# A four-layer graph network on one core: the first layer written out tile by tile, with the adjacency work begun behind the load of x

## The reference

```python
node_att = softmax(x @ node_w, axis=0)
h = x @ edge_w
e = where(adj > 0, h @ h.T, -9e15)
output = adj * (node_att * softmax(e, axis=1)) @ (x @ weight) + bias
```

## Time and profile before

| | us |
|---|---|
| median of 3 runs | 870.79 (870.46 to 871.27) |
| the profiled execution, its own time | 870.08 |
| its span in the trace | 868.3 |
| PE busy | 792.3 (91%) |
| DVE busy | 460.1 (53%) |
| ACT busy | 334.0 (38%) |
| POOL busy | 113.0 (13%) |
| mean granted TensorE clock | 0.977 |

### The profile page before, as it was taken

The page is one execution under the profiler, slowest core; times in us unless marked ns, Lnnn a source line. Parts: engine busy times, 40 slices in busy tenths (PEclk is TensorE's granted clock), DMA queues, the critical chain, the costliest instruction groups (busy, mean ns, idle before and its releaser), DMA issues.

```text
span 868.3 us, 12739 instructions
## 1 busy us (share of the span) xinstructions
PE 792.3 (91%) x4264; PEld 521.0 (60%) x4264; DVE 460.1 (53%) x956; ACT 334.0 (38%) x531; POOL 113.0 (13%) x232
## 2 busy tenths in 40 slices
PE   5948899999969999999997999999998999998997
PEld 5936566666548687768683564556654455465343
DVE  4663667667757768787876347312226021111655
ACT  3455555555425445454554124313335131222200
POOL 1010111111254001010101112000000100000343
PEclk9979999999978999999999999999999999999999
DMA  4149999999920000000002000000000000000011
GB/s 127 35 105 231 215 231 227 231 232 235 190 49 1 13 1 2 1 0 0 0 0 73 7 0 1 1 0 0 0 0 25 1 1 0 0 0 1 18 36 43
DMA packets 114863, 50.61 MB, mean 58 GB/s; under 512 B 103568, under 2 KB 109840, under 8 KB 114832
## 3 DMA queue, kind: packets, MB, share of 16 engines
q1 hardware_dynamic: 114832, 50.22, 25.3%
HBM read 22.95 MB, written 2.10 MB: 29 GB/s over the span
## 4 chain that ended last, share of the span: by engine, by line
PE 45%; issue 24%; SPq 8%; DMA 6%; ACT 6%; DVE 6%; POOL 4%; ACTq 0%; POOLq 0%; DVEq 0%
PE ps L633 10%; PE ps L753 10%; PE ps L731 8%; PE ps L781 7%; DMA adjf<-in_adj 5%; SPq L337 5%; PE ps L762 3%; PE ps L718 3%; SPq L327 2%; PE ps L522 2%; ACT em L819 2%; POOL x L464 2%; DVE em L1076 1%; ACT adjb L814 1%; PE ps L546 1%
## 5 line engine op out<-in xcount | busy, mean ns | idle before, releaser
L633 PE MATMUL ps<-adjT,x 128*128 (+1 forms) x768 | 173.5, 380 | 7.4 <-DVE x L1285 3.8
L633 PEld LDWEIGHTS ps<-adjT,x 128*128 128x128 f16 x768 | 71.6, 98 | 92.9 <-issue 5.6
L573 PE MATMUL ps<-sup,supf 128*128 128x512 f16 x256 | 85.8, 385 | 2.8 <-DMA supf<-pl 2.8
L658 PE MATMUL ps<-H_hi,es_hi 128*128 128x258 f32 x256 | 76.4, 298 | 9.1 <-DVE es_lo L1024 6.0
L1024 DVE TENSOR_TENSOR hh_lo<-hf,hh_hi 128x512 fp32r<-128x512 f32 x32 | 22.2, 692 | 116.6 <-ACT hf L970 116.6
L753 PE MATMUL ps<-adjT,G 128*128 x384 | 83.6, 379 | 0.4 <-ACT hf L970 0.4
L562 PE MATMUL ps<-hT_hi,hst_hi 128*128 128x512 f32 x128 | 54.2, 423 | 22.6 <-DVE mx L1076 14.4
L658 PE MATMUL ps<-H_hi,es_lo 128*128 128x258 f32 x256 | 72.5, 283 | 0.0
L658 PE MATMUL ps<-H_lo,es_hi 128*128 128x258 f32 x256 | 72.3, 283 | 0.0
L575 PE MATMUL ps<-sup,supf 128*128 128x256 f16 x256 | 70.6, 276 | 0.0
L753 PEld LDWEIGHTS ps<-adjT,G 128*128 128x128 f16 x384 | 37.2, 98 | 45.4 <-issue 0.9
(11 more groups left out here) (203 smaller groups left out, 1480.6 us busy)
## 6 DMA issues: line engine op xcount, KB each, us to landing
adjf<-in_adj SPq DMA_DIRECT2D x32, 512.0 KB, 4.7
x<-in_x SPq DMA_DIRECT2D x4, 512.0 KB, 8.2
out<-adjf SPq DMA_DIRECT2D x16, 128.0 KB, 1.7
adjf<-in_L_gnn_W SPq DMA_DIRECT2D x1, 1024.0 KB, 6.2
W1f<-in_L_gnn_W SPq DMA_DIRECT2D x1, 512.0 KB, 3.6
adjf<-in_L_gnn_W SPq DMA_DIRECT2D x1, 512.0 KB, 3.7
we<-in_L_gnn_edge_w SPq DMA_DIRECT2D x1, 256.0 KB, 3.8
w0x<-in_L_gnn_weight SPq DMA_DIRECT2D x1, 256.0 KB, 4.0
```

Source lines behind the costliest of these rows:

```text
L573: ins = mm(bank(6 + u), PT(HI, u)[:, jt, :], sup[:, jt, :], start=(jt == 0), stop=False, skip_group_check=True)
L633: ins = mm(bank(4 + f), x16[:, part, jt, f * P:(f + 1) * P], adjT[:, jt, bass.ds(b * CB, CB)], start=(jt == 0 and part == HI), stop=(jt == ...
L658: ins = mm(bank(k, D + 2), es[p][:, jt % RE, k * P:(k + 1) * P], H[q][:, jt, :], start=(jt == 0 and (p, q) == (HI, HI)), stop=(jt == T - 1 ...
```

## The change

- P0 is reordered: transposes and h of a block alternate, so that a block's h follows when its x has landed; the scores of row 0 stand ahead of the 16 support groups, the scores of row 1 behind them.
- x is loaded ahead of the support weights, the node column and the bias; only `we` (for h) stands between its first and second quarter.
- The adjacency loads are issued right behind x, no longer after the 32 groups. ACT casts rows 0 and 1 behind the h groups, row 2 behind the support groups, and from then on row t+3 in row t. `adjb` has four rows (AB) instead of two, `ph` and `pl` one each instead of two.
- The staging copies of h on POOL are gone: S(t) reads its stationary side from hT itself.
- PT has room of its own. `supf` and the transposed x lie in what are the later blocks of adjT, so the adjacency turns from row 4 on wait for the scaled support.
- adjT is [128, B, T, 512], block by block, for all layers.
- The loops of layer 0 are written out on all engines; the last aggregation loops over blocks of four tiles instead of pairs.

Shapes and the list of the first groups:

```diff
+    AB = 4
...
+    P0 = [(what, b, f) for what, b in (("turn", 0), ("turn", 1), ("h", 0), ("turn", 2), ("h", 1), ("turn", 3), ("h", 2),
+                                       ("h", 3)) for f in range(KD)]
...
-        adjT = sb(ctx, "adjT", [P, T, N], BF16)
+        before = ExitStack()
+        sb(before, "first_block", [P, T, CB], BF16)
+        supf = sb(before, "supf", [P, T, D])
+        xT0 = pair(before, "xT0", [P, KD, N])
+        before.close()
+        adjT = sb(ctx, "adjT", [P, B, T, CB], BF16)
...
+        turned = sb(lay0, "turned", [P, 4, T, P], F16)
...
-        ph, pl = (sb(main0, name, [P, 2, N], F16) for name in ("ph", "pl"))
-        adjb = sb(main0, "adjb", [P, 2, N], BF16)
+        ph, pl = (sb(main0, name, [P, N], F16) for name in ("ph", "pl"))
+        adjb = sb(main0, "adjb", [P, AB, N], BF16)
```

SP:

```diff
                 if c == 0:
-                    sp.dma_start(we[:, :, :], w_tiles(edge_in)).then_inc(w0_landed, 16)
-                    sp.dma_start(w0x[:, :, 0:D], w_tiles(w0_in)).then_inc(w0_landed, 16)
-                    sp.dma_start(w0x[:, :, D:D + 1], w_tiles(node_in)).then_inc(w0_landed, 16)
-                    sp.dma_start(brow[:, :], vec_row(b0_in)).then_inc(w0_landed, 16)
+                    sp.dma_start(we[:, :, :], w_tiles(edge_in)).then_inc(we_landed, 16)
+            sp.dma_start(w0x[:, :, 0:D], w_tiles(w0_in)).then_inc(w0_landed, 16)
+            sp.dma_start(w0x[:, :, D:D + 1], w_tiles(node_in)).then_inc(w0_landed, 16)
+            sp.dma_start(brow[:, :], vec_row(b0_in)).then_inc(w0_landed, 16)
...
+            def turn_adj(t):
...
                 sp.wait_ge(adj_cast, 2 * t + 2)
+                if t >= TB:
+                    sp.wait_ge(sup_lo, TB)
+                sp.dma_start_transpose(adjT[:, t // TB, :, t % TB * P:(t % TB + 1) * P], adjb[:, t % AB, :]) \
+                    .then_inc(adjT_landed[t % AB], 16)
+
+            def turn_p(t, part):
+
+                sp.wait_ge((p_hi, p_lo)[part], 2 * t + 2)
+                wait_from(sp, pv_mm, t - 1)
+                sp.dma_start_transpose(PT(part, t % 2), (ph, pl)[part][:, :]).then_inc(PT_landed[part], 16)
...
-            sp.wait_ge(p0_lo, P0_GROUPS)
             load_adj(0)
             load_adj(1)
-            transpose_adj(0, 0)
-            sp.wait_ge(sup_lo, TB)
...
+            turn_adj(0)
+            load_adj(2)
+            turn_adj(1)
+            load_adj(3)
+            turn_adj(2)
+            turn_p(0, HI)
+            turn_p(0, LO)
+            turn_p(1, HI)
+            load_adj(4)
+            turn_adj(3)
+            load_adj(5)
+            turn_p(1, LO)
+            turn_adj(4)
+            for t in range(2, T):
+                turn_p(t, HI)
+                turn_p(t, LO)
+                if t + 4 < T:
+                    load_adj(t + 4)
+                if t + 3 < T:
+                    turn_adj(t + 3)
```

PE (`group0(n)` is group n of P0 or, from P0_SUP on, a support group):

```diff
-                            ins = mm(bank(c), hst[p][:, u, k, :], hT[q][:, k, c * CB:(c + 1) * CB],
+                            ins = mm(bank(c), hT[p][:, k, t * P:(t + 1) * P], hT[q][:, k, c * CB:(c + 1) * CB],
...
-            scores(0, 0, range(B))
-            scores(1, 1, range(B))
+            for n in range(P0_SUP):
+                group0(n)
+            scores(0)
+            for n in range(P0_SUP, P0_GROUPS):
+                group0(n)
+            scores(1)
+            pe.wait_ge(p0_lo, P0_GROUPS)
             pe.wait_ge(sup_lo, TB)
...
+            for t in range(2, T):
+                scores(t)
+                weighted(t - 2)
+            weighted(T - 2)
+            weighted(T - 1)
```

ACT:

```diff
+            def cast(t):
+
+                if t == 2:
+                    act.wait_ge(p0_lo, P0_GROUPS)
+                if t >= AB:
+                    act.wait_ge(adjT_landed[t % AB], 16 * (t // AB))
+                    act.wait_ge(fill_ready, t - AB + 1)
...
+            for n in range(P0_SUP):
+                group0(n)
+            cast(0)
+            cast(1)
+            for n in range(P0_SUP, P0_SUP + 2):
+                group0(n)
+            exp_row(0)
+            for n in range(P0_SUP + 2, P0_SUP + 6):
+                group0(n)
+            p_high(0)
+            for n in range(P0_SUP + 6, P0_GROUPS):
+                group0(n)
+            cast(2)
             act.wait_ge(node_neg, 1)
             run(nl[:, :], nl[:, :], ACT.Exp, bias=nst[:, 2:3], accum_out=nst[:, 3:4]).then_inc(node_exp, 1)
-            round0(0, 0, 0)
             act.wait_ge(scale_ready, 1)
             for c in range(TB):
...
+            exp_row(1)
+            p_high(1)
+            cast(3)
+            cast(4)
+            for t in range(2, T):
+                exp_row(t)
+                p_high(t)
+                if t + 3 < T:
+                    cast(t + 3)
```

DVE:

```diff
+            for n, (what, b, f) in enumerate(P0):
+                if n == P0_SUP - 2:
+                    dve.wait_ge(w0_landed, 48)
...
             maxima(0, 0)
+            for t in range(T):
+                n = P0_SUP + t
+                dve.wait_ge(p0_hi, n + 1)
...
+            nc.vector.reduce_max(g1[:, 0:1], smax[:, :], AX_X).then_inc(tmax_ready, 1)
+            p_low(0, 0)
+            dve.wait_ge(node_gmax, 1)
+            ts(nst[:, 2:3], nst[:, 1:2], -1.0, None, ALU.mult).then_inc(node_neg, 1)
             scale_of(1)
+            maxima(1, 1)
+            for c in range(TB):
...
+            p_low(1, 1)
...
+            for t in range(2, T):
+                round0(t)
```

Every reader of adjT, here one of them:

```diff
-                                 adjT[:, jt, bass.ds(b * CB, CB)], start=(jt == 0 and part == HI),
+                                 adj(b, jt), start=(jt == 0 and part == HI),
```

More of the change, by code:

```diff
@@ L438, in _ @@
             nc.gpsimd.partition_all_reduce(nst[:, 4:5], nst[:, 3:4], P, RADD).then_inc(node_sum, 1)
[L439 removed]
             bias_x(0, 0)
[L441 removed]
             bias_x(1, 1)
[L443 to L450 removed]
+            for t in range(T - 2):
                 norm_factor(t, t % 2)
@@ L528, in _, with group0 @@
             pe.wait_ge(const_ready, 3)
-            for n in range(P0_GROUPS):
+            def group0(n):
                 if n >= 4:
@@ L550, in _, with scores @@
                     ins = project(bank(to, D + 2), xT0, slice(t * P, (t + 1) * P), w0s, D + 2)
                 ins.then_inc(p0_mm, 1)
-            def scores(t, u, banks):
-                pe.wait_ge(h_staged, 2 * (t + 1))
-                for c in banks:
+            def scores(t):
+                if t == 0:
+                    pe.wait_ge(p0_lo, P0_SUP)
+                for c in range(B):
                     if c % 2 == 0:
@@ L683, in _ @@
             pe.wait_ge(H_ready, 2)
-            for u in range(2):
-                pe.wait_ge(adjT_landed[u], 8 * T)
+            for k in range(AB):
+                pe.wait_ge(adjT_landed[k], 16 * (T // AB))
             block1(0)
@@ L752, in hidden2 @@
                     for part in (HI, LO):
-                        ins = mm(bank(4 + o), g16(jt, part, o * P, P), adjT[:, jt, bass.ds(b * CB, CB)],
+                        ins = mm(bank(4 + o), g16(jt, part, o * P, P), adj(b, jt),
                                  start=(jt == 0 and part == HI), stop=(jt == T - 1 and part == LO))
@@ L761, in _ @@
                     for part in (HI, LO):
-                        ins = mm(bank(4 + o), g16(jt, part, o * P, P), adjT[:, jt, 0:CB],
+                        ins = mm(bank(4 + o), g16(jt, part, o * P, P), adj(0, jt),
                                  start=(jt == 0 and part == HI), stop=(jt == T - 1 and part == LO))
@@ L780, in out3 @@
                         pe.wait_ge(c3_lo, T + jt + 1)
-                    ins = mm(bank(u), adjT[:, jt, bass.ds(t * P, P)], f16[:, jt, :], start=(jt == 0),
+                    ins = mm(bank(u), adjT[:, bass.ds(b, 1), jt, k * P:(k + 1) * P].rearrange("p a c -> p (a c)"), f16[:, jt, :], start=(jt == 0),
                              stop=(jt == T - 1))
                 ins.then_inc(o3_mm, 1)
-            out3(0, 0)
-            out3(1, 1)
-            with pe.Fori(1, T // 2) as i:
-                for u in range(2):
-                    out3(2 * i + u, u)
+            for k in range(TB):
+                out3(0, k)
+            with pe.Fori(1, B) as b:
+                for k in range(TB):
+                    out3(b, k)
         @block.scalar
@@ L797, in _, with group0 @@
             run = nc.scalar.activation
-            for n in range(P0_GROUPS):
+            def group0(n):
                 act.wait_ge(p0_mm, n + 1)
-                b, f, t = n // KD % B, n % KD, n - 4 * B
-                to = (xT0[HI][:, f, b * CB:(b + 1) * CB] if n < 2 * B else
-                      hT[HI][:, f, b * CB:(b + 1) * CB] if n < 4 * B else supf[:, t, :])
-                run(to, bank(4 + n % 4, CB if n < 4 * B else D), ACT.Copy).then_inc(p0_hi, 1)
-            def cast(t, u, used):
-                wait_from(act, adjT_landed[u], 16 * used)
-                wait_from(act, fill_ready, t - 1)
+                if n < P0_SUP:
+                    what, b, f = P0[n]
```

(23 more changed lines are left out.)

219 lines of the change are left out of this document (80 added, 139 removed).

## The result

The kernel after takes 860.37 us (median of 4 runs, 858.82 to 860.67) against 870.62 (869.48 to 871.27) for the kernel before on the same chip: ratio 0.9873, interval 0.9855 to 0.9891, so 1.3% faster, 10.3 us. The forecast was 846, its range 840 to 857: right in sign, but the gain is under half of the one forecast, and the time lies outside the range. The profiled execution took 860.67, its span is 858.9.

What follows compares the result with a forecast made beforehand. Layer 0 was held to run at its DMA's rate, PE 5% to 10% behind full. Next layer at 223.3 instead of 250.66 gains 27.4, less 1.0 clock and 1.5 DMA: 24.9, so 870.8 becomes 846 us, range 840 to 857.

Steps and rivals of the forecast that it cites:

- Start: Kernel start: x's second quarter arrives at 6.5 us and the scores of row 0 begin at 24.0 instead of 38.4.
- Support, S(1) and the stall before S(2): Layer 0: support groups end at 42.9, row 1's scores at 48.5; PE idles 7.1 us; row 2's scores start at 55.6.
- The extra 1.0 for a fallen clock between the support groups: Row 1's scores: 1.0 us allowed, bounds 0 and 5.6, in case gaps between support groups lower PE's clock.
- Rival C: Layer 0 start: ACT's order or load 1 delays row 2's scores to near 64; time 855 us; chance 0.15.
- Rows 2 to 15: Layer 0 rows: PE sets 10.9 us a row, DMA adds 1.5 in all (bounds 0 and 4.4).
- 5 us of DMA against 10.9: Last rows of layer 0: with loads and adjacency turns done ahead, DMA needs 5 us against PE's 10.9.
- rival B: Layer 0 rows: DMA, in SP's fixed order, still sets them; 857.3 us, or 850 at even 11.44 a row; chance 0.16.
- The stronger form: Layer 0 rows stay at 12.07 us each, next layer at 237.2, time 857.3.
- The bound of 10.8 us a row: DMA time of a layer 0 row: transposes at 212 GB/s 7.4 us plus loads at 307 GB/s 3.4 us.
- End: End of layer 0: row 15's scores to next layer take 24.7 us, before 29.5; the 2.80 wait for transposed P goes.
- Unrolled code: Layer 0 rows 2 to 15: straight-line PE instructions cost 0.
- rival D: Layer 0: fetching straight-line code through full DMA engines costs 34 us, making the kernel slower at 880; chance 0.05.

Runs made afterwards that it cites:

- the second run: The kernel after, unchanged, run again in the last group of experiments: 858.77 us, ratio 0.9871 to the kernel before.
- the gate: Kernel after, with x's third and fourth quarters issued only once the first and second have landed: 856.86 us, ratio 0.9845 to the kernel before.
- the quarter run: Kernel after, loading only a quarter of each adjacency row from row 6 on (output not the reference's): 848.82 us, ratio 0.9753 to the kernel before.
- The first experiment: Kernel after, with row 1's low part of P turned right behind its high part, ahead of load 4: 859.06 us, ratio 0.9874 to the kernel before.
- the early transposes: Kernel after, with P of row 0 turned ahead of load 3 and adjacency turn 2, row 1's low part early: 855.01 us, ratio 0.9833 to the kernel before.

## Why the prediction was wrong, step by step

All times are those of the profiled runs; the forecast has the next layer at 223.3 + 1.0 + 1.5 = 225.8, it came at 241.24, 15.4 us later. That is 2.6 at the start, 6.2 in rows 2 to 15 and 7.6 at the end, less 1.0 that wasn't needed.

**Start: mis-sized by 2.6.** x's second quarter was put at 6.5 and came at 9.22, so S(0) came at 26.57 for 24.0. In the second run it was 7.9 and 24.63, so this miss is in good part one of the execution. The estimate counted only `we` and that quarter, while SP issues the other two quarters by 3.34. That these take bandwidth from it fits the gate, with which the second quarter was never later than 7.00; one run without the gate had it at 6.98 too, so it is likely, not shown.

**Support, S(1) and the stall before S(2): right.** S(0) to S(1) 19.04 for 18.9, S(1) to S(2) 12.62 for 12.7, a stall of 6.99 for 7.1, and S(2) to W(0) 6.92 for 7.0 at a granted clock of 0.79 (part of it at 1.2 GHz). The gaps between the support groups lie elsewhere than stepped through: 0.55 and 0.83 us of idle behind groups 4 and 6, both released by DVE's reduction, where the text had one behind group 6 and one behind group 10, by ACT. That their sum came out right is luck in part, and so are the 6.92 behind the stall: in the second run S(2) takes 8.14 to W(0), at the same idle time before it. The extra 1.0 for a fallen clock between the support groups wasn't used: it was 1.00 in every window up to 48 us. Rival C, the lost head start, did not happen: S(2) at 58.23, 5.9 us earlier.

**Rows 2 to 15: the first failed step.** "the slack of a row (7 us at first) can swallow all of it", and of bounds 0 and 4.4 the text takes 1.5. S(2) to S(15) took 150.7 us for 143.0 + 1.5: 6.2 missing. PE's own full row was overrated beside it, 10.9 for 10.71 measured, some 2 us over eleven rows, which hides as much of the miss. The text had the right number in hand: 2.62 million bytes a row at 222 GB/s, 11.8 us, and 13 x 2.62 / 0.223 = 153 us for the stretch. The trace moves 150.68 x 223 = 33.6 million bytes in it, 12.8 rows. PE's 143.0 us were the smaller of the two, and the slack it counted is only a delay: at 10.71 us a row the transfers fall behind (98 to 162, no idle on PE) until the room is used up, and then the rows go at 11.64 (162 to 209). Whether the pace of the transfers is that of the engines or that of SP's issues stays open, as said at the quarter run. The slower rows then last to S(15), since by then the last load has only just gone out; the "5 us of DMA against 10.9" came too late to help. LO(1) did land after W(1) was due (W(1) at 79.71 for 73.4, through two issues of 5.1 us in SP's queue), and with the half clock that its 3.69 us of idle brought W(1) and S(4) were 6.1 us later against S(2) than forecast. The first experiment shows that this isn't a second loss: without it the stretch takes the same 150.68. The other seven runs with all the bytes and PE's order give 147.0 to 151.7, the one with fewer bytes 144.8. So of rival B, at 0.16 beside 0.62 for rows bound by PE, one half came true: the transfers set the rows. The other half, "in SP's fixed order", did not; two changes of that order gave nothing. Nor did its even 11.44 a row from S(4): it was 121.5 / 11 = 11.04 in the mean, first 10.71 and then 11.64, with the stretch before S(4) 6.1 us longer. That B's 850 plus the 2.6 of the start and the 7.6 of the end makes 860.2 is therefore luck in part. (The stronger form's 857.3 leaves out the 1.0 for the clock that the sum has; with it it is 858.3.)

The bound of 10.8 us a row from 212 and 307 GB/s, measured apart, was too low for the mixture: the kernel after holds 223 to 227 GB/s at a share of 1.09, and that is 11.6 us. The Trainium skill, "DMA: Bandwidth & Descriptors", Latency and other measured facts, gives a DMA transpose 261 GB/s; an estimate by it has a row need 1.57/261 + 1.05/307 = 9.4 us, and PE would set every row. The traces do not agree with it: 212 GB/s while transposes ran alone.

**End: the second failed step, and the larger, mis-sized by 7.6.** S(15) to the next layer took 32.3 for 24.7. "The transposes now have 7 us of room, so that wait goes" took the middle rows' 21.8 us from the start of one row's scores to its W, in which two more tiles of PE's work lie. Behind S(15) there is only W(13) and W(14), 2 x 5.2 = 10.4 us from its end at 214.5, and the turned `pl` lands at 229.8, 15.3 later. That is more than the 14 of the text because DVE started late. Its low parts of rows 14 and 15:

```profile
212.89 2.36 DVE L1091 SCALAR_TENSOR_TENSOR pl<-em,ph 128x1024 f16<-128x1024 f32 x2 [0.73 <-DMA turned<-pl]
...
222.09 2.36 DVE L1091 SCALAR_TENSOR_TENSOR pl<-em,ph 128x1024 f16<-128x1024 f32 x2 [0.73 <-ACT ph L829]
```

That of row 14 waits for the turn of row 13, and the maxima of row 15 stand behind it. Of the 7.6 us, 3.8 are the wait before W(15), 0.8 that before W(14), and most of the rest the half clock after them (W(15) takes 8.0 us from its start to its end for 5.4 at full clock). Two rows of `pl` take 3.6 us off (1.8 of them clock), fewer bytes 3.3, and neither brings it near 24.7. What stays before W(15), 2.4 to 3.1 us, is the chain of the last row itself, which had cost 2.80 before already; moving S(15) forward does not shorten the end. Whether halving the last turn would was not tried.

**Unrolled code: right at 0.** The page's row of the instruction queue:

```profile
q8 instruction: 22, 0.36, 0.2%
```

It was 17 packets. From 98.11 to 162.35 PE is busy 64.24 of 64.24 in straight-line code at a DMA share of 1.09, so rival D is refuted. The Trainium skill, "Runtime: NRT & Kernel Launch", Instruction fetch mechanics, has straight-line code streamed ahead; this trace agrees. adjT in blocks and the last aggregation cost nothing either: 617.66 for 617.63.

## What to carry to other kernels

Where two resources each need nearly the time of a row, take the larger total over the whole stretch, bytes by the rate measured for that mixture (here 153 for 150.7 us), and let slack between rows count only once, as a delay, never per row. Room for a transfer is to be counted anew for the last tile of a pipeline, where the work of the following tiles no longer stands between. When the transfers set the time, reordering them inside the full stretch gained nothing here; fewer bytes did, and filling the idle stretch ahead of the limit shortened the rows by up to 3 us. Where one queue issues everything, read its busy share beside that of the DMA engines: here both were full, and a cut in bytes relieved both.

## What the runs showed of the hardware

- A transfer was often late when others were issued right behind it: PE had x's second quarter at 6.98 to 9.22 us (half of ten runs at 7.9 or later) when two more quarters followed at once, and at 6.67 to 7.00 in the three runs that held them back.
- Issuing a DMA transpose right behind a 1 MB load on the same queue took 4.8 to 6.0 us, behind another transpose 1.3 to 3.5. The long issue belongs to whichever transpose stands behind the load (4.5 to 5.4 us for P's high part when the order was changed), and it falls to 2.4 to 3.0 us when the load has a quarter of the bytes. The instructions behind it in SP's stream wait that long.
- 7.0 us of idle before S(2) brought TensorE from 2.4 to 1.2 GHz in all thirteen runs with the new order, and S(2), 5.6 us at full clock, then took 6.9 to 8.3 to W(0). 5.6 and 3.5 us before an early S(15) did the same. Idle times of 1.5 to 1.7 us before a W never did. From 2.0 to 3.9 us it went either way. W(15), 5.4 us long at full clock, took 8.0 behind 3.83 us of idle, but also 7.0 and 5.35 behind 3.83 in two other runs (the gate, and the early transposes); 7.04 behind 2.80 in the kernel before and behind 2.39 in the quarter kernel; and 5.36 behind 2.98. Behind 1.99 and 2.17 us a W took 7.04, behind 2.15 it took 5.35. So such a wait can cost up to 2.6 us more than its own length, and single executions differ by that much.
